# Graph attention on one core: the order of TensorE's transposes, and of the last graph's work, is changed

## The chip, the core and the metric

The kernel runs on one core of a Trainium2 chip. The metric is the time on the device in microseconds (us), lower is better. A core has TensorE (PE in the rows, its weight loads PEld), VectorE (DVE), ScalarE (ACT), GpSimd (POOL) and SyncE (SP, which here only issues DMAs), each with its own queue of instructions, worked through in order. Semaphores order the engines among each other.

## The reference

For each of 32 graphs of 256 nodes with 256 features and 8 heads of 32, all in float32:

```python
q, k, v = (proj(Wq, bq), proj(Wk, bk), proj(Wv, bv))
scores = jnp.einsum('bhqd,bhkd->bhqk', q, k) * SCALE
mask = (adj_matrix + bond_matrix)[:, None, :, :]      # both are adj: 2 * adj
attn = jax.nn.softmax(scores * mask, axis=-1)
ctx = jnp.einsum('bhqk,bhkd->bhqd', attn, v)
y = jnp.einsum('bse,fe->bsf', ctx, Wo) + bo           # ctx with heads side by side
x = _layernorm(x + y, axis=-1)
```

## The kernel before

The work is a software pipeline over the 32 graphs. Each engine has a function `step(g)`, called for g = 0 to 31, and a tail that is written out by hand behind it. In step g TensorE makes the scores of graph g, while the sums over the values belong to graph g − 2 and the output projection to graph g − 3.

A graph's eight heads are two groups of four; group n is 2g or 2g + 1. For a group:

- TensorE makes the scores (`rows`, L265: 16 matmuls of 32 rows each, four heads side by side in the array) into four PSUM banks `row_bank`.
- VectorE multiplies them by the mask, writes `probs` and the row maxima `top` (`reduce_rows`, L524). GpSimd negates the maxima (`lower_tops`, L934), and ScalarE takes the exponential with them as bias, and sums the rows (`exp`, L729).
- The sums over the values need the probabilities turned. Three heads of a group are turned in 32 by 32 blocks on VectorE (`box`, L537) and carried across partitions by four DMAs from SyncE (`carry_boxes`, L209) into `carried`. The fourth head, "the head" in this text, is turned on TensorE (`turn_probs`, L282: four transposes into `turn_bank`) and moved to `turned_probs` by ScalarE (`move_turned`, L737).
- `weigh_v` (L405: 32 matmuls of 32 columns each) sums over the values into `ctx_bank`. It waits for the boxes of both groups and for both moved heads.

The sums of the exponentials become shares: VectorE takes the reciprocal (`divide`, L545), GpSimd spreads them over 512 columns (`spread_shares`, L870, into `wide`), TensorE turns them (`turn_shares`, L367, four transposes, also into `turn_bank`), and ScalarE copies them to `inverse` (`copy_inverse`, L743). VectorE multiplies sums and shares (`scale_context`, L552), GpSimd cuts the product into a high and a low part (`cut_context`, L878 and L880), and TensorE projects it (`project_out`, L422, 12 matmuls) into `out_bank`. VectorE adds the residual (`add_residual`, L558; GpSimd has added the bias to it, `add_bias`, L887), takes the statistics (L566, L572), and GpSimd normalises (`make_scale`, L894 to L903, `normalise`, L910). ScalarE issues the store (`store`, L788) and the loads of masks and residuals (`load_masks`, `load_x`).

Beside that TensorE projects two graphs ahead: per step two of the four projections for k and q of a pair (`project_kq`, L334, 6 matmuls, into `proj_bank`, read by ScalarE in `read_kq`, L757), and v of the next graph (`project_v`, L352). There are 16 pairs, so that steps 30 and 31 have no `project_kq`.

`turn_bank` has four users in a row: the second-group head of graph g − 1 and the first-group head of graph g, each followed by ScalarE's move, and the shares, followed by ScalarE's copy. `turn_probs` and `turn_shares` wait for the move or the copy before them (L278, L279, L364). So TensorE's order in a step is scores, projection, output projection, shares, sums, head, scores, projection, v, head.

For the last graph nothing is carried. All its eight heads are turned on TensorE (`turn_last`, L287), moved by ScalarE or VectorE (`move_last`), summed half by half, scaled, cut, projected and normalised in halves (`scale_last`, `high_last`, `low_last`, `project_last`, `add_last`, `normalise_last`). Both engines' copies are counted by `last_moved_act` and `last_moved_dve`, for which `weigh_v(LAST)` waits.

Of the kernel before, what the change touches and what calls it, by code (L numbers as in the profile page):

```python
# [35 lines left out]
LAST = B - 1  # L36
# [4 lines left out]
def build(nc, x, x_t, adj, adj_t, wq, wk, wv, wo, bq, bk, bv, bo, out):  # L41
    ctx = ExitStack()
    with ctx:
# [206 lines left out]
        def _(pe):  # L250
# [121 lines left out]
            def weigh_v(g):  # L372
# [6 lines left out]
                if g == LAST:  # L379

                    pe.wait_ge(last_moved_act, 3)
                    pe.wait_ge(last_moved_dve, 5)
                else:

                    wait(pe, ctx_ready, g)
                    pe.wait_ge(moved, 2 * g + 2)
                    for n in range(T * g, T * g + T):
                        pe.wait_ge(carried_in[n % 4], 64 * (n // 4 + 1))
# [79 lines left out]
            def step(g):  # L468
# [7 lines left out]
                if g == 1:  # L476
                    make_bias()
                if is_graph(g - 3):
                    project_out(g - 3)
                if is_graph(g - 2):  # L480
                    turn_shares(g - 2)
                    weigh_v(g - 2)
                turn_probs(2 * g - 1)
# [25 lines left out]
        def _(dve):  # L509
# [172 lines left out]
            for g in range(B):  # L682
                step(g)
            aggregate(LAST - 3)
            for j in (2, 3):
                move_last(0, j)
# [3 lines left out]
            move_last(1, 2)  # L690
            add_residual(LAST - 2)
# [20 lines left out]
        def _(act):  # L712
# [96 lines left out]
            def step(g):  # L809
                ahead = g // 2 + 1  # L810
                for s in range(H):
                    n, j = 2 * g + s // J, s % J
                    if s == 0 and is_graph(g - 2):
                        copy_inverse(g - 2)
# [14 lines left out]
                    if s == (6 if g < LAST else 1) and is_graph(g):  # L829
                        load_x(g)  # L830
                    if s == (3 if g > 0 else 4) and is_pair(ahead):
                        read_kq(ahead, 2 * (g % 2) + 1)
# [4 lines left out]
                    if s in (3, 4) and g == LAST:  # L837
                        move_last(0, s - 3)
                    if s == 7 and is_pair((g + 1) // 2 + 1):
                        read_kq((g + 1) // 2 + 1, 2 * ((g + 1) % 2))  # L840
# [3 lines left out]
            move_last(1, 3)  # L844
            store(LAST - 4)
            copy_inverse(LAST)
# [8 lines left out]
        def _(pool):  # L855
# [81 lines left out]
            def step(g):  # L937
# [3 lines left out]
                if is_graph(g - 1):  # L941
                    spread_shares(g - 1)
                    if g % 2 == 0:
                        add_bias((g - 1) // 2, 1)
                if is_graph(g - 2):
                    cut_context(g - 2)
                lower_tops(2 * g + 1)
                if g % 2 == 1:
# [9 lines left out]
            add_bias(LAST // 2, LAST % 2)  # L958
            make_scale(LAST - 3)
            normalise(LAST - 3)  # L960
            spread_shares(LAST)
            cut_context(LAST - 1)
            make_scale(LAST - 2)
# [48 lines left out]
```

## Time and profile before

| | |
|---|---|
| time before, median of 3 runs | 404.72 us |
| lowest and highest | 403.47 and 408.22 us |
| the profiled execution, its own time | 409.81 us |
| its span, first to last instruction | 408.0 us |
| mean granted TensorE clock | 0.988 |
| busy: PE, PEld, DVE, ACT, POOL | 94%, 72%, 89%, 89%, 67% |
| mean DMA rate | 226 GB/s |

The profiled execution is longer than the median of the three. Its rows have times in microseconds from the span's start. A timeline row has the start, the length from the first start to the last end of what it merges, engine, source line, operation, tile written and tiles read, the shape and the count; in brackets the idle time of the engine before it and what ended it. TensorE's matmuls are pipelined, so that the blocks overlap by some 0.1 to 0.2 us and their starts tell more than their ends.

### The profile page before, as it was taken

To read this page: it belongs to the slowest core of one execution; us is meant where nothing else is said; L and a number is where in the kernel's file an instruction comes from. 1 tells how busy PE (TensorE), PEld (TensorE's weight loads), DVE (VectorE), ACT (ScalarE), POOL (GpSimd) and SP (SyncE) were. 2 spreads that over 40 slices of the span, in tenths; PEclk is the share of its full clock that TensorE was granted. 3 is DMA by queue.
4 is the path that set the end of the run, shared out by engine and by line. 5 is a ranking of instruction groups with operands and counts; after the bars stand their busy time and mean duration, and the time that the engine had idled before them with its cause. 6 is when DMAs were issued, how large, how long until landed. Compare 5 with 4: busy or idle time off the path is not lost.

```text
span 408.0 us, 12272 instructions
## 1 busy us (share of the span) xinstructions
PE 382.6 (94%) x3628; PEld 293.5 (72%) x3628; DVE 364.4 (89%) x1336; ACT 362.4 (89%) x1223; POOL 272.8 (67%) x507
## 2 busy tenths in 40 slices
PE   8999999999999999999999999899999899996872
PEld 7766777877777777777777776677777677775632
DVE  4998899999899999899999988899999899999655
ACT  4699999999899999999999998899999899998810
POOL 3245647777586777768777775768777587475583
PEclk9999999999999999999999999999999999999968
DMA  8478888888999998889899889998988888887603
GB/s 271 135 199 246 223 236 241 247 216 224 270 269 241 255 258 233 254 228 272 241 259 243 225 204 247 261 250 250 261 240 217 220 246 225 224 223 193 174 26 104
DMA packets 65428, 92.30 MB, mean 226 GB/s; under 512 B 8529, under 2 KB 48722, under 8 KB 65362
## 3 DMA queue, kind: packets, MB, share of 16 engines
q1 hardware_dynamic: 47426, 66.35, 62.3%
q10 hardware_dynamic: 17936, 25.17, 19.5%
q8 instruction: 29, 0.48, 0.4%
q14 instruction: 37, 0.30, 0.2%
HBM read 26.22 MB, written 8.39 MB: 85 GB/s over the span
## 4 chain that ended last, share of the span: by engine, by line
PE 48%; SPq 22%; DVE 8%; DMA 8%; ACT 5%; issue 5%; POOL 2%; DVEq 0%; POOLq 0%
SPq L209 13%; PE proj_bank L334 11%; PE ctx_bank L405 9%; SPq L218 9%; PE row_bank L265 9%; DMA carried<-boxes 8%; PE out_bank L422 5%; PE out_bank L352 5%; PE turn_bank L282 5%; ACT probs L729 4%; DVE probs L524 4%; DVE boxes L537 2%; PE turn_bank L367 2%; PE turn_bank L454 1%; ACT kq L757 1%
## 5 line engine op out<-in xcount | busy, mean ns | idle before, releaser
L729 ACT ACTIVATE probs<-probs,low_top 128x256 f32<-128x256 f32 x512 | 254.6, 506 | 4.3 <-POOL low_top L934 4.3
L524 DVE CUSTOM_DVE_ANT_0 probs<-row_bank,adj_rows 128x256 f32<-128x256 f32 x512 | 181.1, 420 | 22.0 <-issue 12.6
L537 DVE STREAM_TRANSPOSE boxes<-probs 128x1536 f32<-128x1536 f32 x62 | 108.9, 1757 | 0.0
L729 ACT ACTIVATION_READ_ACCUMULATOR probs<-probs,low_top 128x1 f32 x512 | 100.5, 196 | 0.0
L334 PE MATMUL proj_bank<-xt_parts,w_parts 128*128 128x512 f32 x360 | 99.7, 412 | 0.0
L334 PEld LDWEIGHTS proj_bank<-xt_parts,w_parts 128*128 128x128 f32 x360 | 62.9, 188 | 30.8 <-issue 19.6
L934 POOL TENSOR_SCALAR low_top<-top 128x4 f32<-128x4 f32 x128 | 25.3, 198 | 79.3 <-issue 36.0
L265 PE MATMUL row_bank<-kq 32*128 32x256 f32 x1024 | 73.3, 400 | 1.5 <-DVE top L524 1.5
L405 PE MATMUL ctx_bank<-carried,v_boxed 128*32 128x256 f32 x744 | 59.6, 383 | 8.3 <-DMA carried<-boxes 8.1
L265 PEld LDWEIGHTS row_bank<-kq 32*128 32x128 f32 x1024 | 46.4, 184 | 13.7 <-issue 11.8
L422 PEld LDWEIGHTS out_bank<-w_parts,ctx_parts 128*128 128x128 f32 x372 | 48.8, 191 | 5.1 <-issue 2.7
L352 PEld LDWEIGHTS out_bank<-w_parts,xt_parts 128*128 128x128 f32 x384 | 50.3, 190 | 2.9 <-issue 0.3
L352 PE MATMUL out_bank<-w_parts,xt_parts 128*128 128x256 f32 x384 | 51.3, 283 | 0.0
L422 PE MATMUL out_bank<-w_parts,ctx_parts 128*128 128x256 f32 x372 | 50.3, 285 | 1.1 <-issue 1.1
L405 PEld LDWEIGHTS ctx_bank<-carried,v_boxed 128*32 128x32 f32 x744 | 29.6, 109 | 28.1 <-issue 14.0
L737 ACT COPY turned_probs<-turn_bank 128x512 f32<-128x512 f32 x62 | 36.2, 585 | 7.6 <-PE turn_bank L282 7.4
L524 DVE DVE_READ_ACCUMULATOR2_ANT top<- 128x1 f32 x512 | 42.8, 84 | 0.0
L880 POOL TENSOR_TENSOR ctx_parts<-context,ctx_parts 128x512 fp32r<-128x512 f32 x31 | 40.2, 1298 | 2.5
L887 POOL TENSOR_TENSOR xr<-xr,bias 128x512 f32<-128x512 f32 x32 | 41.0, 1281 | 0.0
L864 POOL TENSOR_TENSOR xt_parts<-xt,xt_parts 128x512 fp32r<-128x512 f32 x30 | 38.9, 1297 | 2.6
L282 PE MATMUL turn_bank<-ident,probs 128*128 128x128 f32 x248 | 39.1, 280 | 1.2 <-ACT probs L729 0.7
L282 PEld LDWEIGHTS turn_bank<-ident,probs 128*128 128x128 f32 x248 | 27.3, 141 | 14.5 <-ACT probs L729 10.9
(85 smaller groups left out, 436.9 us busy)
## 6 DMA issues: line engine op xcount, KB each, us to landing
carried<-boxes SPq DMA_DIRECT2D x248, 192.0 KB, 3.9
xt<-in_x_t SPq DMA_DIRECT2D x32, 256.0 KB, 4.7
adj_rows<-in_adj ACTq DMA_DIRECT2D x32, 256.0 KB, 3.5
xr<-in_x ACTq DMA_DIRECT2D x32, 256.0 KB, 4.4
v_boxed<-v SPq DMA_DIRECT2D x124, 64.0 KB, 3.4
out<-result ACTq DMA_DIRECT2D x31, 256.0 KB, 4.5
w_whole<-in_wk ACTq DMA_DIRECT2D x2, 128.0 KB, 3.5
w_whole<-in_wq SPq DMA_DIRECT2D x1, 256.0 KB, 4.2
```

Source lines behind the costliest of these rows:

```text
L209: sp.dma_start(carried[:, g % 2, c, i].rearrange("p h f -> p (h f)"), boxes[D * i:D * (i + 1), n % BOXES].rearrange("p j h f -> p j (h f)" ...
L265: last = nc.tensor.matmul(row_bank[j][:, t * S:(t + 1) * S], kq[own, pair % 2, 2 * c + 1, b * S + t * P:b * S + (t + 1) * P], kq[own, pair ...
L282: last = nc.tensor.transpose(turn_bank[:, c * S + t * P:c * S + (t + 1) * P], probs[:, (J * n + J - 1) % RING, t * S + c * P:t * S + (c + ...
L334: last = nc.tensor.matmul(proj_bank[:], w_parts[:, a, which, t, c * P:(c + 1) * P], xt_parts[:, pair % 2, b, t, :], start=(half_ == 0 and ...
L352: last = nc.tensor.matmul(out_bank[:, tile * E:(tile + 1) * E], xt_parts[:, (n // 2) % 2, a, t, nodes], w_parts[:, c, 2, t, :], start=(til ...
L405: last = nc.tensor.matmul(place.rearrange("p (u i q) -> p u i q", u=T, i=J), values[:, (g // 2) % 2, g % 2, t, o * D:(o + 1) * D], tile, s ...
L422: last = nc.tensor.matmul(out_bank[:, n * E:(n + 1) * E], ctx_parts[:, g % 2, a, f, nodes], w_parts[:, b, 3, f, :], start=(n == 0 and i == 0),
L524: last = nc.vector.tensor_tensor_reduce(probs[:, h % RING, t * S:(t + 1) * S], row_bank[j][:, t * S:(t + 1) * S], adj_rows[:, (g // 2) % 2 ...
L537: nc.vector.transpose(boxes[:, n % BOXES].rearrange("p a h (f q) -> p (h f) a q", q=D), probs[:, first:first + BOXED, :].rearrange("p h (f ...
L729: last = nc.scalar.activation(tile, tile, ACT.Exp, bias=low_top[:, g % 2, J * c + j, t:t + 1], accum_out=sums[:, g % 2, t, j * T + c:j * T ...
L880: nc.gpsimd.tensor_tensor(low, context[:], high.bitcast(F32), ALU.subtract).then_inc(ctx_low, 1)
L887: nc.gpsimd.tensor_tensor(tile, tile, bias[:].unsqueeze(1).to_broadcast([P, T, E]), ALU.add).then_inc(x_ready, 1)
```

## The change

Three things change, and nothing of what is computed.

TensorE's step: `turn_shares(g - 2)` moves ahead of `project_out(g - 3)`, and `turn_probs(2 * g - 1)` ahead of `weigh_v(g - 2)`. The order is then scores, projection, shares, output projection, head, sums, scores. ScalarE follows: `copy_inverse` is issued at the end of the step before, behind the last exponentials and ahead of `read_kq`, where it was behind `read_kq`.

The loads and biases of the last residuals: `load_x(LAST)` is issued in step 30, and both `add_bias` of the last pair come in step 31 ahead of `cut_context(g - 2)` and the second tops.

The tail: VectorE turns to `move_last(0, 2)` and the residual of graph 29 earlier, and `move_last(1, 2)` goes from VectorE to ScalarE, so TensorE waits for four copies of each. GpSimd spreads the last shares and cuts the context of graph 30 ahead of `normalise(LAST - 3)`.

```diff
@@ tensor: weigh_v
-                    pe.wait_ge(last_moved_act, 3)
-                    pe.wait_ge(last_moved_dve, 5)
+                    pe.wait_ge(last_moved_act, 4)
+                    pe.wait_ge(last_moved_dve, 4)
@@ tensor: step
+                if is_graph(g - 2):
+                    turn_shares(g - 2)
                 if is_graph(g - 3):
                     project_out(g - 3)
+                turn_probs(2 * g - 1)
                 if is_graph(g - 2):
-                    turn_shares(g - 2)
                     weigh_v(g - 2)
-                turn_probs(2 * g - 1)
                 rows(2 * g + 1)
@@ vector: tail
+            move_last(0, 2)
             aggregate(LAST - 3)
-            for j in (2, 3):
-                move_last(0, j)
+            add_residual(LAST - 2)
+            move_last(0, 3)
             for j in (0, 1):
                 move_last(1, j)
             divide(LAST)
-            move_last(1, 2)
-            add_residual(LAST - 2)
             scale_context(LAST - 1)
@@ scalar: step
-                    if s == 0 and is_graph(g - 2):
-                        copy_inverse(g - 2)
...
-                    if s == (6 if g < LAST else 1) and is_graph(g):
+                    if s == 6 and g < LAST:
                         load_x(g)
+                    if s == 7 and g == LAST - 1:
+                        load_x(LAST)
...
+                    if s == 7 and is_graph(g - 1) and g < LAST:
+                        copy_inverse(g - 1)
                     if s == 7 and is_pair((g + 1) // 2 + 1):
                         read_kq((g + 1) // 2 + 1, 2 * ((g + 1) % 2))
@@ scalar: tail
-            move_last(1, 3)
+            for j in (2, 3):
+                move_last(1, j)
+            copy_inverse(LAST)
             store(LAST - 4)
-            copy_inverse(LAST)
@@ gpsimd: step
+                if g == LAST:
+                    for b in range(2):
+                        add_bias(LAST // 2, b)
                 if is_graph(g - 2):
                     cut_context(g - 2)
                 lower_tops(2 * g + 1)
-                if g % 2 == 1:
+                if g % 2 == 1 and g < LAST:
                     add_bias((g - 1) // 2, 0)
@@ gpsimd: tail
-            add_bias(LAST // 2, LAST % 2)
             make_scale(LAST - 3)
-            normalise(LAST - 3)
             spread_shares(LAST)
             cut_context(LAST - 1)
+            normalise(LAST - 3)
             make_scale(LAST - 2)
```

## Rows read from the trace of the kernel before

**Rows 1.** The waits from 50 to 350 us: engine and line, total, times, longest.

```profile
PE ctx_bank L405 <- DMA carried<-boxes: 6.6, 8, 1.4
```

**Rows 2.** The waits of SyncE's DMA queue in the same stretch.

```profile
SPq L209 <- DVE boxes L537: 16.8, 19, 1.9
```

**Rows 3.** The timeline of TensorE in step 29, from first scores to the next step's.

```profile
348.83 1.15 PE L265 MATMUL row_bank<-kq 32*128 32x256 f32 x16
349.90 1.68 PE L334 MATMUL proj_bank<-xt_parts,w_parts 128*128 128x512 f32 x6
351.42 1.58 PE L422 MATMUL out_bank<-w_parts,ctx_parts 128*128 128x256 f32 x12
352.84 0.60 PE L367 MATMUL turn_bank<-ident,wide 128*128 128x128 f32 x4
353.37 1.27 PE L405 MATMUL ctx_bank<-carried,v_boxed 128*32 128x256 f32 x18
...
354.92 0.39 PE L405 MATMUL ctx_bank<-turned_probs,v 128*32 128x256 f32 x2
355.24 0.66 PE L282 MATMUL turn_bank<-ident,probs 128*128 128x128 f32 x4
355.82 1.15 PE L265 MATMUL row_bank<-kq 32*128 32x256 f32 x16
356.90 1.65 PE L334 MATMUL proj_bank<-xt_parts,w_parts 128*128 128x512 f32 x6
...
360.36 1.15 PE L265 MATMUL row_bank<-kq 32*128 32x256 f32 x16
```

**Rows 4.** The timeline of ScalarE in the same stretch, without the exponentials.

```profile
350.08 0.58 ACT L737 COPY turned_probs<-turn_bank 128x512 f32<-128x512 f32 x1
...
352.54 0.68 ACT L757 ACTIVATE kq<-proj_bank,b_k 128x512 f32<-128x512 f32 x1
353.48 0.59 ACT L743 COPY inverse<-turn_bank 128x512 f32<-128x512 f32 x1 [0.26 <-PE turn_bank L367]
...
358.59 0.69 ACT L757 ACTIVATE kq<-proj_bank,b_q 128x512 f32<-128x512 f32 x1
```

**Rows 5.** The timeline of GpSimd in the tail.

```profile
386.34 1.11 POOL L910 TENSOR_SCALAR result<-y,scale 128x256 f32<-128x256 f32 x2
387.41 1.28 POOL L887 TENSOR_TENSOR xr<-xr,bias 128x512 f32<-128x512 f32 x1
...
391.46 0.61 POOL L870 COPY wide<-shares 128x512 f32<-128x512 f32 x1
```

**Rows 6.** The timeline of TensorE in step 31 and the tail.

```profile
376.42 1.27 PE L405 MATMUL ctx_bank<-carried,v_boxed 128*32 128x256 f32 x18 [1.30 <-DMA carried<-boxes]
...
384.71 0.60 PE L304 MATMUL turn_bank<-ident,probs 128*128 128x128 f32 x4
385.15 1.69 PE L304 MATMUL row_bank<-ident,probs 128*128 128x128 f32 x12
...
388.63 0.66 PE L304 MATMUL row_bank<-ident,probs 128*128 128x128 f32 x4
392.12 1.11 PE L367 MATMUL turn_bank<-ident,wide 128*128 128x128 f32 x4 [2.83 <-POOL wide L870]
```

**Rows 7.** Windows: stretch, its length, busy of the five engines, PEclk, DMA share, GB/s.

```profile
392.00:398.00 6.00, 5.88 (x42) 3.36 (x43) 1.41 (x4) 1.40 (x3) 4.28 (x9) 0.50 0.00 0
```

**Rows 8.** The timeline of TensorE in step 2: the head.

```profile
36.68 0.63 PE L282 MATMUL turn_bank<-ident,probs 128*128 128x128 f32 x4 [0.52 <-ACT inverse L743]
```

**Rows 9.** The timeline of ScalarE in step 2: the copy of the shares.

```profile
35.94 0.60 ACT L743 COPY inverse<-turn_bank 128x512 f32<-128x512 f32 x1
```

**Rows 10.** The timeline of VectorE in the tail.

```profile
387.68 1.28 DVE L580 COPY carried<-row_bank 128x512 f32<-128x512 f32 x2
388.87 0.24 DVE L545 RECIPROCAL shares<-sums 128x16 f32<-128x16 f32 x1
...
399.17 0.69 DVE L558 TENSOR_TENSOR y<-out_bank,xr 128x512 f32<-128x512 f32 x1 [0.97 <-PE out_bank L422]
```

## What the change does to the time: the prediction

> **What bounds the kernel now.** I read the page first, for the engines' shares, then the waits of the middle 300 us, then the timeline of one undisturbed step, engine by engine, then the timeline of the end. TensorE, VectorE and ScalarE are all nearly full by the page, so what counts is which of them the others wait for. In the middle TensorE itself waits for one thing that the profile names, the boxes carried by DMA: 6.6 us in 8 waits between 50 and 350 us [rows 1]. SyncE's queue in its turn waited for the boxes 19 times in that stretch, 16.8 us in all [rows 2], so in most of the 25 steps it caught up with its work. It is close to full, and a late box is a queue's lateness, which comes and goes.
>
> [rows 3] is one whole step (`g` = 29) without such a wait. The starts of TensorE's blocks: first scores 348.83, projection 349.90, output projection 351.42, turned shares 352.84, sums 353.37, turned head 355.24, second scores 355.82, and the next step at 360.36. A step is 11.53 us, and no gap stands in it that another engine made: TensorE sets the pace. ScalarE runs just behind [rows 4]: it is through with the head's exponentials at 352.54, reads a projection, stands 0.26 us until the turned shares are there, and copies them from 353.48 to 354.07. It meets TensorE again at 358.59, when the second projection has ended (355.82 + 1.08 + 1.65 = 358.55). So from the second scores to the copy of the shares it keeps a fixed distance to TensorE.
>
> The end is another regime. The last graph's shares are spread on GpSimd at 391.46, after two residual biases and two normalisations [rows 5]; TensorE stands for 2.83 us and goes on at 392.12 [rows 6] at half the clock, 0.50 from 392 to 398 us [rows 7], which is 1.2 GHz.
>
> **Part 1: the order on TensorE in a step.** Nothing is computed more or less; blocks change places. What changes is the switch between matmuls on the whole array and those on a quarter of it (scores 32*128, sums 128*32). Four transposes cost 0.53 us ahead of the sums (353.37 − 352.84) and 0.58 between sums and scores (355.82 − 355.24) [rows 3], but 0.44 when a whole-array block follows (385.15 − 384.71) [rows 6]. Before, from the projection to the second scores: 1.52 + 1.42 + 0.53 + 1.87 + 0.58 = 5.92. After, with shares, output projection, head, sums: 1.52 + 0.44 + 1.42 + 0.53 + 1.87 = 5.78. That is 0.14 us less a step. Its weak term is the last, sums straight into scores, which the trace does not have. The sums go in 8 rounds of four, (354.92 − 353.37) / 7 = 0.22 apart, and the head comes 0.32 after the last round's start. If the scores follow at the sums' own pitch, the 1.87 is 1.77 and the gain 0.24. I take 1.87: the scores' weights need all 128 columns, which the last sums still use.
>
> The Trainium skill, "TensorEngine Tiling (Array Packing)", section Tiling Modes, says that a change of tiling mode, not merely of tile, drains TensorE. By it sums into scores is still a change of mode: 1.87 stands, and the step has one such change less; without the rule it would be 1.77.
>
> **Part 2: who must now be in time.** The turned head goes into the bank that the shares were in, so it waits for ScalarE's copy of them. Before, the sums (1.87 us) lay between and hid this; now the output projection does, 1.42 us. In the old step's times TensorE is ready for the head at 349.90 + 1.52 + 0.44 + 1.42 = 353.28. ScalarE has the copy right behind the exponentials now, ahead of the projection's read: 352.54 + 0.59 = 353.13 [rows 4], and TensorE starts 0.14 after such a copy has ended (35.94 + 0.60 to 36.68) [rows 8, 9]: 353.27. That is a tie, and as ScalarE's distance to the second scores is fixed, it is one in every step. A weight load that has to wait is not drawn ahead either, 0.05 us (0.58 against 0.53). Bounds: 0 and 0.15 us a step in 27 steps; I take 0.5 us in all, near the lower end. A gain is excluded, since it is a wait.
>
> The shares, 1.42 us earlier, need the move of the head before: 350.08 + 0.58 = 350.66, against 351.42 [rows 3, 4]: 0.76 us to spare, nothing. ScalarE's projection read comes behind the copy, but the 0.26 of standing goes, and the exponentials queued behind both start earlier than now. VectorE's product of sums and shares gets its sums 0.4 us later; it is behind a transpose then, and ahead of the mask of the second scores, which needs scores that end later still. GpSimd's cut and SyncE's queue get no new wait in front of them.
>
> **Part 3: the carried boxes.** The sums start 0.44 us later behind the projection than now, and the step is 0.14 shorter. Boxes are pinned to the second scores of two steps before, so the allowance grows by 0.30 us. Eight waits at 0.30 are 2.4 us, ten over the run 3.0; nothing if SyncE's queue, which has 0.14 us less a step to catch up, gives it back. I take 1.2.
>
> **Part 4: the start.** In step 2 ScalarE is still a microsecond behind and there is no output projection. TensorE does the sums first, then the head waits for the copy until 36.68 [rows 8, 9]. After, the copy is ahead of the projection's read, some 0.57 earlier, head at 36.11, then 0.53 + 1.87 until the scores: 38.51, against 36.68 + 0.58 = 37.26. It is 1.25 later, of which step 3 gives back some, since ScalarE has then caught up. Cost 1.1 (bounds 0 and 1.3).
>
> **Part 5: the end.** Steps 30 and 31 have no projection, so the shares wait for the move and the head for the copy, in the open; against that the sums of step 31, which stand 1.30 us for boxes now [rows 6], come late enough not to. I put the last scores 0.5 earlier than now. On GpSimd both residual biases (1.28 us each) lie ahead of the last tops; the load that the second needs is issued a step earlier, so it is there. The normalisation of graph 27 ends at 386.34 + 1.11 = 387.45 now [rows 5], and at 387.45 − 1.28 − 0.5 = 385.65 after. VectorE's residual (0.69) waits for it, then come three copies (1.28 for two) and the reciprocal (0.24) [rows 10]: 385.65 + 0.6 + 1.9 + 0.2 = 388.35 at the most, 388.1 with the overlaps of the pipeline. The normalisation of graph 28 no longer stands ahead of the spread: + 0.1 + 0.61 = 388.8. TensorE's last head ends at 388.63 + 0.66 − 0.2 = 389.1 [rows 6]. So the shares turn at 389.1 instead of 392.12: 3.0 us. TensorE then never stands for 2.8 us, so the granted clock should stay at 2.4 GHz. ScalarE copies the last head (0.58 and 0.14) until 389.8, sums 1.87, output projection 1.42 and 0.3 until VectorE takes it: 393.4, against 399.17 now [rows 10]. From the shares to that residual it was 7.05 us and is 4.3: 2.75 more. Behind it all is as now. Together 5.75 us; 3.0 if the clock falls all the same.
>
> **Sum.** 1.1 − 27 × 0.14 (3.8) − 1.2 + 0.5 − 5.75 = −9.15 us against the profiled execution's span of 408.0: 398.9. That execution took 409.8 us by its own time, 5 us over the median of 404.72. I put the difference to waits for boxes, so the median has fewer of them to save: 0.5 instead of 1.2. 404.72 − 8.45 = 396.3, rounded to 396.5.
>
> **Rivals.** (a) *ScalarE's copy is late.* For it the tie above; against it that TensorE itself fixes the copy's place. At 0.15 us a step the steps gain nothing: 3.5 more, 400.0. Chance 0.13. (b) *The DMA side keeps the pace.* Each step carries the same bytes. SyncE's idle time is 16.8 us in 25 steps [rows 2], 0.67 a step, of which 0.14 is taken; so it has room. If it gives back all that the steps save, the end is left and half of the start: 404.7 − 5.75 + 0.5 = 399.5. Chance 0.1. (c) *The clock falls in the tail anyway:* 396.5 + 2.75 = 399.3. Chance 0.1. (d) *Sums flow into scores:* 27 × 0.10 less, 393.8. Chance 0.08. (e) *Slower: the head's wait for the copy grows.* If shares and copy come later than the rows say, every step pays on TensorE with all engines behind it. 8.45 / 27 = 0.31 us a step cancels the gain; 0.46 makes it 1% slower, 408.8. For it: VectorE and ScalarE have under 0.5 us a step to absorb anything. Against it: 0.31 is twice my upper bound. Chance 0.04. The forecast has 0.55.
>
> **How the numbers follow.** Under 1% a measurement of this kernel can't tell from no change. The predicted time is the forecast's; the range reaches below (d), and over (a), (b) and (c): 393.2 to 401.2. Faster by over 1% is below 400.7: the forecast, (c), (d), most of (a) and (b), 0.84. Slower by over 1% has 0.04, within 1% the remaining 0.12.
>
> **What would show it.** In an undisturbed step: a period of 11.39 instead of 11.53; the head right behind the output projection; no idle time ahead of the copy of the shares; sums to scores 1.87 (or 1.77). Fewer than 8 waits for boxes in the same stretch. A wait of TensorE for `inverse` in each step shows (a) or (e). In the tail: shares turned 3 us sooner, seen from the start of step 30, and a granted clock of 1.00 to the last matmul. I would be wrong above all by block lengths that no row has, and by VectorE's chain from the normalisation to the reciprocal.

## The result: slower, by 2.6%

| | before | after |
|---|---|---|
| median of 4 runs each, us | 406.26 | 417.5 |
| lowest to highest, us | 403.47 to 408.22 | 412.85 to 418.01 |
| profiled execution, time / span, us | 409.81 / 408.0 | 417.26 / 415.5 |

The ratio after to before is 1.0256, with a 95% interval of 1.0154 to 1.0359, so it is slower beyond the noise. Medians here and below take all runs of a kernel, while ratios leave out runs over 1.5% above the fastest of their kernel, so the two can differ by over 1%. The forecast was 396.5 us.

The page of after shows the change of regime at once. First line: span. Then the engines' busy time and the chain that ended last, share by engine:

```profile
span 415.5 us, 12272 instructions
PE 378.0 (91%) x3628; PEld 293.3 (71%) x3628; DVE 365.8 (88%) x1335; ACT 360.2 (87%) x1224; POOL 272.9 (66%) x507
...
SPq 55%; PE 21%; issue 5%; DMA 5%; ACT 5%; DVE 4%; POOL 3%; DVEq 0%; POOLq 0%
```

SyncE's DMA queue now holds 55% of that chain, where it held 22% before and TensorE 48%. The waits from 50 to 350 us (engine and line, total, times, longest):

```profile
ACT kq L757 <- PE proj_bank L334: 27.4, 24, 3.9
...
PE ctx_bank L405 <- DMA carried<-boxes: 18.1, 17, 2.0
```

and those of SyncE's queue in the same stretch:

```profile
SPq L209 <- DVE boxes L538: 2.4, 4, 1.2
```

TensorE waits for carried boxes 17 times and 18.1 us instead of 8 times and 6.6 [rows 1]. SyncE waited for the boxes 19 times, 16.8 us, before [rows 2]; now 4 times, 2.4 us. So it hardly ever catches up: what it is late with goes on into the next step.

Yet a step without such a wait is the one that was forecast. TensorE in step 29 (start, length, engine, line, operation, output and inputs, shape, count), the counterpart of [rows 3]:

```profile
360.93 1.15 PE L265 MATMUL row_bank<-kq 32*128 32x256 f32 x16
362.01 1.66 PE L334 MATMUL proj_bank<-xt_parts,w_parts 128*128 128x512 f32 x6
363.50 0.60 PE L367 MATMUL turn_bank<-ident,wide 128*128 128x128 f32 x4
363.86 1.67 PE L422 MATMUL out_bank<-w_parts,ctx_parts 128*128 128x256 f32 x12
365.36 0.62 PE L282 MATMUL turn_bank<-ident,probs 128*128 128x128 f32 x4
365.92 1.27 PE L405 MATMUL ctx_bank<-carried,v_boxed 128*32 128x256 f32 x18
...
367.78 1.15 PE L265 MATMUL row_bank<-kq 32*128 32x256 f32 x16
...
372.32 0.93 PE L265 MATMUL row_bank<-kq 32*128 32x256 f32 x12
```

Its period is 372.32 − 360.93 = 11.39 us, and sums to scores take 367.78 − 365.92 = 1.86. But over steps 6 to 28 the period is 12.31 us in the mean, from 11.38 to 15.07; it was 11.85 before. Step 30 starts at 372.32 instead of 360.36: 12.0 us lost. From there to the end it takes 43.2 us instead of 47.6: 4.5 won back. That is the +7.5 of the spans; by the medians it is 11.2, since before's profiled execution was longer than its median by 3.5.

**What moved that the forecast had not followed.** ScalarE in the same step, its DMA issues among its work (ACTq), the counterpart of [rows 4]:

```profile
364.64 0.57 ACT L743 COPY inverse<-turn_bank 128x512 f32<-128x512 f32 x1
364.75 0.41 ACTq L788 DMA_DIRECT2D out<-result  x1
365.11 0.69 ACT L757 ACTIVATE kq<-proj_bank,b_k 128x512 f32<-128x512 f32 x1
366.22 0.33 ACTq L716 DMA_DIRECT2D adj_rows<-in_adj  x1
367.65 0.58 ACT L737 COPY turned_probs<-turn_bank 128x512 f32<-128x512 f32 x1
```

The issue of the masks' load (256 KB) stands in ScalarE's queue behind `move_turned(2 * g - 1)`, so it goes out once TensorE has turned that head. Before, the rows of step 29 were

```profile
353.49 0.40 ACTq L788 DMA_DIRECT2D out<-result  x1
...
355.94 0.34 ACTq L716 DMA_DIRECT2D adj_rows<-in_adj  x1
```

with first scores at 348.83 [rows 3]: store at 4.66 us in the step, load at 7.11. After, with first scores at 360.93: 3.82 and 5.29. Over steps 6 to 28 the medians are 4.66 and 7.11 before, 4.24 and 5.30 after. The load comes 1.8 us earlier, right behind the store of 256 KB. From issue to landing (minimum, median, maximum, between 50 and 350 us) the load took 3.1, 3.5, 4.0 us before and the store 3.8, 4.6, 5.3. After, first the load, then the store:

```profile
DMA to landing us min/median/max: 4.6/6.0/7.2
```

```profile
DMA to landing us min/median/max: 4.7/5.9/7.1
```

What SyncE does meanwhile depends on how late it is. Where it is on time it issues the values (`v_boxed`, L218) in this stretch: over steps 6 to 28 they begin at 5.0 us of a step before and 4.8 in e10 below (medians), and are through at 8.7 and 7.6. In after they begin at 7.2 and end at 11.2, because the queue is late with the boxes ahead of them. The store's and the load's transfers, issued at 4.24 and 5.30 and 6 us long, reach from the boxes' issues into the values'. SyncE in step 15 of after, whose first scores are at 187.45:

```profile
186.48 3.06 SPq L209 DMA_DIRECT2D carried<-boxes  x4
189.58 1.12 SPq L200 DMA_DIRECT2D xt<-in_x_t  x1
190.80 3.13 SPq L209 DMA_DIRECT2D carried<-boxes  x4
194.03 4.13 SPq L218 DMA_DIRECT2D v_boxed<-v  x4
198.25 3.09 SPq L209 DMA_DIRECT2D carried<-boxes  x4
201.39 0.68 SPq L200 DMA_DIRECT2D xt<-in_x_t  x1
```

and ScalarE's issues in the same step:

```profile
192.39 0.44 ACTq L788 DMA_DIRECT2D out<-result  x1
...
193.19 0.69 ACTq L716 DMA_DIRECT2D adj_rows<-in_adj  x1
```

Store and load are issued among the boxes, right ahead of the values' issues, which take 4.13 us for four, and SyncE goes from one group to the next without a pause. Over steps 6 to 28 issuing the values took 3.54 us a step before and 3.87 after, the boxes 6.28 and 6.94: a microsecond more a step in a queue that had 0.67 us to spare by [rows 2]. With the load of `xt` it is 10.44 us a step before and 11.47 after, which is more than after's undisturbed step of 11.39: such a queue cannot keep up. The Trainium skill, "DMA: Bandwidth & Descriptors", section Issuing engines are not separate DMA queues, says that transfers of all issuing engines run on the same DMA engines and interleave. The trace agrees as to the landing times; that also the issue on another queue gets longer is what the trace adds.

### The profile page after: what moved, and what is told of

The parts are those of the page before. It is cut to its first block, busy times and chain, and to the rows that moved or that the text cites. A ratio compares the mean times of both kernels' runs of the same rounds, so it can differ in the third digit from the quotient of the medians.

```text
span 415.5 us, 12272 instructions
## 1 busy us (share of the span) xinstructions
PE 378.0 (91%) x3628; PEld 293.3 (71%) x3628; DVE 365.8 (88%) x1335; ACT 360.2 (87%) x1224; POOL 272.9 (66%) x507
## 4 chain that ended last, share of the span: by engine, by line
SPq 55%; PE 21%; issue 5%; DMA 5%; ACT 5%; DVE 4%; POOL 3%; DVEq 0%; POOLq 0%
SPq L209 33%; SPq L218 19%; PE ctx_bank L405 5%; PE proj_bank L334 5%; PE row_bank L265 4%; ACT probs L729 4%; DMA carried<-boxes 4%; SPq L200 3%; PE out_bank L352 2%; PE out_bank L422 2%; DVE probs L525 2%; PE turn_bank L282 1%; DVE boxes L538 1%; DMA xt<-in_x_t 1%; POOL result L913 1%
## 5 line engine op out<-in xcount | busy, mean ns | idle before, releaser
L525 DVE CUSTOM_DVE_ANT_0 probs<-row_bank,adj_rows 128x256 f32<-128x256 f32 x512 | 181.1, 419 | 15.6 <-PE row_bank L265 11.9
L405 PE MATMUL ctx_bank<-carried,v_boxed 128*32 128x256 f32 x744 | 61.1, 389 | 18.8 <-DMA carried<-boxes 18.7
L937 POOL TENSOR_SCALAR low_top<-top 128x4 f32<-128x4 f32 x128 | 25.3, 197 | 73.1 <-issue 47.7
L405 PEld LDWEIGHTS ctx_bank<-carried,v_boxed 128*32 128x32 f32 x744 | 31.8, 110 | 38.1 <-issue 25.6
L422 PE MATMUL out_bank<-w_parts,ctx_parts 128*128 128x256 f32 x372 | 51.6, 288 | 0.0
L422 PEld LDWEIGHTS out_bank<-w_parts,ctx_parts 128*128 128x128 f32 x372 | 46.0, 189 | 0.4 <-issue 0.4
L757 ACT ACTIVATE kq<-proj_bank,b_q 128x512 f32<-128x512 f32 x30 | 20.6, 688 | 28.5 <-PE proj_bank L334 28.5
L881 POOL CAST ctx_parts<-context 128x512 fp32r<-128x512 f32 x31 | 19.0, 613 | 38.5 <-DVE context L553 38.4
L282 PE MATMUL turn_bank<-ident,probs 128*128 128x128 f32 x248 | 38.1, 276 | 3.4 <-ACT inverse L743 2.6
```

The costliest lines, as they stand in the source:

```text
L282: last = nc.tensor.transpose(turn_bank[:, c * S + t * P:c * S + (t + 1) * P], probs[:, (J * n + J - 1) % RING, t * S + c * P:t * S + (c + ...
L405: last = nc.tensor.matmul(place.rearrange("p (u i q) -> p u i q", u=T, i=J), values[:, (g // 2) % 2, g % 2, t, o * D:(o + 1) * D], tile, s ...
L422: last = nc.tensor.matmul(out_bank[:, n * E:(n + 1) * E], ctx_parts[:, g % 2, a, f, nodes], w_parts[:, b, 3, f, :], start=(n == 0 and i == 0),
L525: last = nc.vector.tensor_tensor_reduce(probs[:, h % RING, t * S:(t + 1) * S], row_bank[j][:, t * S:(t + 1) * S], adj_rows[:, (g // 2) % 2 ...
```

## The experiments

Ratios are to the kernel before in the same sitting, whose medians lay between 403.9 and 406.0 us; intervals are 95%. The sittings were on three chips, and before's own median moves by 2 us between them; so do not read a difference of 2 us between kernels of different sittings. "Moment" is the median time of an issue from its step's first scores; "waits" are TensorE's waits for carried boxes from 50 to 350 us.

### Which part costs

**e3: the end alone**, in the old order of the step.

```diff
@@ vector, scalar, gpsimd: tails; load_x(LAST), add_bias
+  as in the change
@@ tensor: step; scalar: copy_inverse in step
   as before
```

> The kernel before with the change's edits from step 30 on alone: load of the last residual, biases, order of the tail on VectorE, ScalarE and GpSimd. The steps' order on TensorE and ScalarE is that of before. By the two traces the stretch from step 30 to the end is 4.5 us shorter in the changed kernel (43.2 against 47.6): 400 to 402 us. If the tail's gain hangs on the order of the steps, 404 to 406.

Measured: 402.3 us, ratio 0.9922 (0.9875 to 0.997); waits 5.3 us in 6. The new end is worth 3 to 4 us by the times. By the traces it is more: from step 30's start to the end e3 takes 42.0 us, before 47.6; 1.30 of the 5.7 are a wait for boxes in before's step 31 [rows 6].

**e4: the step's order alone**, with the old end.

```diff
@@ tensor: step; scalar: copy_inverse in step
+  as in the change
@@ all tails, load_x, add_bias
   as before
```

> The change's order of a step alone (shares ahead of the output projection, head ahead of the sums, copy of the shares ahead of the projection's read), the tail as before. Both theories: the whole loss is here, 416 to 422 us, more than the changed kernel's own 417.5 less 4.5 for its tail and with some 15 us more than before by step 30.

Measured: 421.75 us, ratio 1.0403 (1.0332 to 1.0475); waits 15.6 us in 11. The loss is in the order of the step, and it is larger than what the new end returns.

**e8: only the shares first**; the head is turned behind the sums again.

```diff
@@ tensor: step
-                turn_probs(2 * g - 1)
                 if is_graph(g - 2):
                     weigh_v(g - 2)
+                turn_probs(2 * g - 1)
```

> The changed kernel with the head turned behind the sums again; the shares stay ahead of the output projection, and ScalarE's copy of them ahead of the projection's read. The turned head comes at about 7 us again, and with it the load of the masks, since ScalarE's queue waits for the head ahead of it. The step is about 11.5 us. Theory A: 400 to 404 us. Theory B, since the step is as long as before: also 400 to 404 us. If the loss comes from the shares' and the copy's place, 412 us or more.

Measured: 403.96 us (median of 10) beside 405.31 before, ratio 1.0068 (1.0013 to 1.0123); the ratio stands on the other side of 1 than the medians, so "about the same" is all that can be said. Waits 3.2 us in 5, masks at 7.11, store at 4.24, shortest period 11.50. The half of the change that moves the head is the half that costs, and with it goes the masks' moment.

**e7: is it that the step is short?** After, with two more transposes in each step, so that SyncE has more time a step and not less.

```diff
@@ tensor: turn_probs, behind the waits
+                if n % 2 == 0 and n > 0:
+                    for c in range(T):
+                        nc.tensor.transpose(turn_bank[:, c * S:c * S + P],
+                            probs[:, (J * n + J - 1) % RING, c * P:(c + 1) * P], ident[:])
```

> The changed kernel with two more transposes on TensorE in each step (they repeat two of the first head's, so the result is the same): a step without waits is 11.6 us instead of 11.39, longer than before's 11.53. Masks and store go out as in the changed kernel. Theory A: nothing is gained, 416 to 420 us. Theory B: SyncE's queue can catch up again, waits for boxes fall to those of before, 402 to 408 us.

Measured: 420.18 us, ratio 1.0416 (1.0306 to 1.0525). An undisturbed step is 11.57 to 11.60 us, longer than before's 11.51, and the waits are still 10.9 us in 11, with store and load at 4.02 and 5.10. The short step by itself is not the cause.

### The moment of the masks' load

**e1: the load one place later** in ScalarE's queue.

```diff
@@ scalar: step
-                    if s == 2 and is_graph(g + 2):
-                        load_masks(g + 2)
+                    if s == 3 and is_graph(g + 2):
+                        load_masks(g + 2)
```

> The changed kernel with one edit: ScalarE issues the load of the masks behind the fourth exponential of a step instead of behind the third. In the changed kernel that load went out 5.3 us after a step's first scores, 1.06 us behind the store; before it was 7.11 us and 2.45 us. Theory A (the load of the masks has moved onto the store, and the two together hold up SyncE's queue): issue at 6.3 to 6.8 us, landing of masks and stores back under 5 us, SyncE's issues of boxes back towards 6.3 us a step, and a time of 397 to 403 us. Theory B (the shorter step leaves SyncE's queue no time to catch up, whatever ScalarE loads): no change, 412 to 418 us.

Measured: 413.35 us, ratio 1.0203 (1.0152 to 1.0254); moment 6.28, waits 11.3 us in 10. Load and store landed after 4.5 and 4.9 us (medians), as theory A had it, and yet the time lies in theory B's range and 10 us over theory A's. The load went only half of the way to 7.1. This run could not decide between the two; e7 and e5 do.

**e5: the load back at its old moment.** ScalarE's queue waits for the sums before it issues it.

```diff
@@ scalar: step
                     if s == 2 and is_graph(g + 2):
+                        if is_graph(g - 2):
+                            act.wait_ge(ctx_made, g - 1)
                         load_masks(g + 2)
```

> The changed kernel, with ScalarE waiting for the sums of the step before it issues the load of the masks. It then goes out about 7.0 us after a step's first scores, as in the kernel before, and later when TensorE waits for boxes, also as before. Theory A (the moment of that load and its distance from the store do the harm; at 6.28 us a third of the loss was gone): waits for boxes near those of before, 398 to 404 us. Theory B (the step of 11.39 us is too short for SyncE's queue): still 410 to 414 us.

Measured: 405.03 us (median of 10), ratio 0.9999 (0.9949 to 1.0048); moment 6.99; waits 6.2 us in 8, SyncE's own 13.3 us in 19. TensorE's order is that of after, and the loss against before is gone; e6, which turned out to be the same kernel in effect, measured 407.85 (ratio 1.0125). At 405 to 408 instead of 417.5 this shows that the loss hangs on when the load goes out. The range of theory A, 398 to 404, was still too low.

**e2: the early load in the old order.**

```diff
@@ scalar: step
-                    if s == 2 and is_graph(g + 2):
+                    if s == 1 and is_graph(g + 2):
                         load_masks(g + 2)
```

> The kernel before with one edit: the load of the masks stands ahead of the move of the turned head, so that it doesn't wait for the head any more. Order of TensorE, tail and all else as before. Theory A: the load goes out about 1 us behind the store as in the changed kernel, masks and stores take 5.5 to 6 us to land, more and longer waits for boxes, 411 to 420 us. Theory B: TensorE's step is as long as before, so 403 to 408 us, as before.

Measured: of ten runs four took 403.1 to 405.3 us and six 411.5 to 420.8; the median is 411.61. The ratio, 0.9977 (0.9926 to 1.0027), goes by the four, and by it the early load costs the old order nothing, where theory A had 411 to 420. Why the six are longer is not shown; before's runs beside them lie between 402.0 and 411.1. In the trace, of a run of 411.53 us, the moment is 5.26 with the store at 4.66, landing takes 5.6 us (median), and the waits are 7.5 us in 11, hardly more than before's 6.6 in 8. So this run does not support the cause. It limits it: that a load at 5.3 near a store costs 12 us is shown in the new order alone, and what of the new order it needs (the store at 4.24 instead of 4.66, or the order itself) is open.

**e9: the load after the values**, at 8 us.

```diff
@@ scalar: step
-                    if s == 2 and is_graph(g + 2):
-                        load_masks(g + 2)
...
+                    if s == 3 and is_graph(g + 2):
+                        act.wait_ge(rows_made, 2 * g + 2)
+                        load_masks(g + 2)
```

> The changed kernel, with the load of the masks issued behind the fourth exponential and only when the second scores are made, about 8.1 us after a step's first scores and 3.9 us behind the store: three transfers of ScalarE's nearly even over the step. If more distance from the store helps further, 399 to 403 us; if what the gate at 7.0 us gave (405.0) was all there is, 403 to 407; if the load must also keep clear of the boxes that SyncE issues from about 8 us on, 408 or more.

Measured: 407.84 us (median of 10), ratio 1.0045 (0.9988 to 1.0102); moment 8.07, waits 5.3 us in 9. A load at 8 us does not do better than one at 6.99 in e5. With the store left at 4.2 some waits stay.

**e11: the same in the old order**, with the new end.

```diff
@@ scalar: step (over e3)
-                    if s == 2 and is_graph(g + 2):
-                        load_masks(g + 2)
...
+                    if s == 3 and is_graph(g + 2):
+                        act.wait_ge(rows_made, 2 * g + 2)
+                        load_masks(g + 2)
```

> The order of a step as before, the tail of the change, and the masks' load issued at about 8.1 us as in the first kernel of this set (3.4 us behind the store at 4.66). Against the tail alone (402.3 us, masks at 7.1 us): 399 to 402 if spacing helps, 402 to 404 if 2.45 us behind the store were enough already.

Measured: 405.28 us (median of 10), ratio 1.002 (0.9972 to 1.0068), against 0.9922 for e3, and over both ranges expected. In the trace, which is of the longest of the ten runs (411.1 us), the load fell at 8.52, the waits are 9.6 us in 15, and the mean period was 12.0. Later is not better for the load in this order either.

### The store

**e6: the store one place later** (over e5).

```diff
@@ scalar: step
-                    if s == 0 and is_graph(g - 5):
+                    if s == 1 and is_graph(g - 5):
                         store(g - 5)
```

> As the run with the gated masks, and the store is issued one head later too (about 5.2 us after the first scores, where the changed kernel has 4.24 and the kernel before 4.66). Theory A in its wider form (each of ScalarE's transfers has to meet few boxes): within 2 us of the gated masks, either way; if the store's 0.4 us is what is left of the loss, 4 us or more faster than it. Theory B: 410 to 414 us.

Measured: 407.85 us, ratio 1.0125 (1.0019 to 1.0231). The store still went out at 4.25, so the edit did not move it: one exponential more ahead of it does not hold the queue. It decides nothing about the store. What it gives is a second measurement of e5's kernel, 3 us over the first, with waits of 9.0 us in 12.

**e10: the store away from the values**, the load left where the change put it.

```diff
@@ scalar: step
-                    if s == 0 and is_graph(g - 5):
-                        store(g - 5)
+                    if s == 3 and is_graph(g - 5):
+                        act.wait_ge(rows_made, 2 * g + 2)
+                        store(g - 5)
```

> The changed kernel, with the masks' load left where the change put it (5.3 us) and the store moved away instead: issued behind the fourth exponential when the second scores are made, about 8.1 us, 2.8 us behind the masks. If the harm is that store and masks stand together, 402 to 407 us. If it is the masks' load at 5.3 us in itself, against SyncE's values and boxes, 414 to 419 us.

Measured: 395.9 us (395.43 to 398.46), ratio 0.9769 (0.9715 to 0.9822). This beats both kernels, and lies under both ranges expected. The chain that ended last, by engine:

```profile
PE 84%; ACT 8%; POOL 3%; issue 2%; DVE 1%; DMA 1%; DVEq 0%; POOLq 0%; ACTq 0%
```

TensorE has no wait for carried boxes left between 50 and 350 us, and SyncE's queue has 26 of its own:

```profile
SPq L209 <- DVE boxes L538: 23.3, 26, 2.0
```

Step 16 (first scores 191.78), ScalarE's issues and then SyncE's:

```profile
197.07 0.33 ACTq L716 DMA_DIRECT2D adj_rows<-in_adj  x1
199.84 0.40 ACTq L788 DMA_DIRECT2D out<-result  x1
```

```profile
193.23 3.22 SPq L209 DMA_DIRECT2D carried<-boxes  x4
196.54 2.58 SPq L218 DMA_DIRECT2D v_boxed<-v  x4
```

The load still goes out among the values, at 5.29 us, but alone; the store follows at 8.06, when they are through. Four values take 2.58 us here, not 4.13; over steps 6 to 28 the values take 2.76 us a step and the boxes 6.64, with `xt` 9.90 in all. Every step from 6 to 28 takes 11.38 to 11.41 us.

**e14: both late and near each other**, load at 6.99 and store at 8.06, in the new order.

```diff
@@ scalar: step (over e10)
                     if s == 2 and is_graph(g + 2):
+                        if is_graph(g - 2):
+                            act.wait_ge(ctx_made, g - 1)
                         load_masks(g + 2)
```

> The changed kernel with the masks' load at 7.0 us (behind the sums) and the store at 8.1 us (behind the second scores), 1.07 us apart as in the changed kernel, but 3 us later in the step. If nearness harms wherever it is, 410 us or more; if it is the store at 4.2 us among SyncE's values, 395 to 399 us.

Measured: 399.08 us, ratio 0.9897 (0.9856 to 0.9939), waits 1.0 us in 3. The two are 1.07 us apart, as in after (1.06), and hardly a wait is left. Of the 3.2 us over e10 about 1.6 are half clock behind a stand in step 2 (last section), which e10's trace does not have. So it is not their nearness by itself that costs, but where in SyncE's round they lie.

**e12: the old order, new end, store at 8.19**, load at its old 7.10; and **e13: the same with the load at 4.68**, the old order's counterpart of e10.

```diff
@@ scalar: step (e12, over e3)
-                    if s == 0 and is_graph(g - 5):
-                        store(g - 5)
...
+                    if s == 3 and is_graph(g - 5):
+                        act.wait_ge(rows_made, 2 * g + 2)
+                        store(g - 5)
@@ scalar: step (e13, over e12)
-                    if s == 2 and is_graph(g + 2):
+                    if s == 1 and is_graph(g + 2):
                         load_masks(g + 2)
```

> The order of a step as before, the change's tail, and the store issued when the second scores are made (8.1 us); the masks' load stays at 7.1 us, so that the two are 1 us apart. If nearness is what harms, 408 us or more; if the store's moment at 4.7 us harms, waits for boxes go and the time is 397 to 400 us.

> As the kernel before this in the set, with the masks' load at 5.3 us too: ScalarE's transfers at the moments of the kernel that took 395.9 us, with the step's order of before and the change's tail. Without waits for boxes step 30 starts at 360.4 - 7.6 = 352.8 us, against 351.4 in that kernel: 397 to 398.5 us, so that the order of the step is worth 1 to 2.5 us. If the new order is what takes the waits away, 402 or more.

Measured: e12 400.6 us (median of 10), ratio 0.9906 (0.9871 to 0.9941), waits 0.9 us in 3. e13 398.65 us, ratio 0.9898 (0.9851 to 0.9944), waits 1.4 us in 3, shortest period 11.51. The late store takes the waits away in the old order too, but what that gains in time against e3 (ratio 0.9922) is not clear of the noise. And e13 beside e10 gives what TensorE's new order is worth when the queue isn't in the way: 2.75 us by the medians, some 5 by the ratios, which come from two sittings, and 3.2 us by the start of step 30 (354.55 against 351.37), of which 1.4 are e13's waits.

Time is the median of all runs, ratio that to before in the same sitting.

| kernel | order | load | store | waits, us | time, us | ratio |
|---|---|---|---|---|---|---|
| before | old | 7.11 | 4.66 | 6.6 | 406.26 | 1 |
| e2 | old | 5.26 | 4.66 | 7.5 | 411.61 | 0.9977 |
| e3 | old, new end | as before | as before | 5.3 | 402.3 | 0.9922 |
| e11 | old, new end | 8.52 | 4.66 | 9.6 | 405.28 | 1.002 |
| after | new | 5.30 | 4.24 | 18.1 | 417.5 | 1.0256 |
| e8 | new, old head | 7.11 | 4.24 | 3.2 | 403.96 | 1.0068 |
| e1 | new | 6.28 | as after | 11.3 | 413.35 | 1.0203 |
| e5 | new | 6.99 | 4.24 | 6.2 | 405.03 | 0.9999 |
| e9 | new | 8.07 | 4.25 | 5.3 | 407.84 | 1.0045 |
| e14 | new | 6.99 | 8.06 | 1.0 | 399.08 | 0.9897 |
| e10 | new | 5.30 | 8.07 | 0 | 395.9 | 0.9769 |
| e12 | old, new end | 7.10 | 8.19 | 0.9 | 400.6 | 0.9906 |
| e13 | old, new end | 4.68 | 8.20 | 1.4 | 398.65 | 0.9898 |

## Why the prediction was wrong

**The step that failed** is the last sentence of part 2: "GpSimd's cut and SyncE's queue get no new wait in front of them." It is true of semaphores. But I had listed what is queued behind ScalarE's copy, which the change moves, and not what is queued behind its move of the turned head, whose moment moves with the head. An issue of 256 KB stands there. Before, the head was turned at 355.24, 6.4 us into the step [rows 3]; after, at 365.36, 4.4 us in. The load follows it, 7.11 to 5.30, and its transfer lies beside SyncE's issues together with the store's. What the runs showed in place of "no new wait" is a queue whose issues took 1 us a step longer, and 18.1 us of waits for boxes instead of 6.6. The trace of before could have told: the issue's moment was there to be read, and that it follows the head is in the code.

**Rival (b) had the right place and the wrong mechanism.** It said that the DMA side keeps the pace, and counted bytes a step and SyncE's idle time, with the lengths of SyncE's issues taken as fixed. The bytes did not change, so on its terms the queue could do no more than give back the steps' gain. What changed was how long SyncE's own issues take when others' transfers lie beside them: 1 us a step more, against 0.67 of slack. Rival (e), the only slower one, put the loss at the head's wait for the copy; that wait is 1.8 us, once, at the start, none between 50 and 350, and 0.8 behind. With 0.04 for slower the text had no room for what happened.

**Part 1 was right.** Undisturbed period 11.38 to 11.41 (11.39 forecast), sums to scores 1.86 (1.87). With it rival (d), sums that flow into the scores at 1.77, falls. Those 27 × 0.14 us are in the kernel; they show in e10, whose steps all take this long.

**Part 2's tie held exactly.** The copy of the shares ends at 364.64 + 0.57 = 365.21, and the head starts at 365.36, 0.15 behind it and right behind the output projection; no idle time ahead of the copy. It costs nothing that can be seen, where I had 0.5. Rival (a) falls.

**Part 3 had the wrong sign.** Forecast: waits for boxes shrink by 1.2 us (0.5 for the median). Measured: idle time ahead of the sums from 8.3 to 18.8 us over the run. The allowance of 0.30 us follows from the blocks' starts; the boxes came later by more.

**Part 4.** The second scores of step 2 came 1.29 us later than before, seen from its first scores (7.86 us against 6.57); the forecast was 1.25, of which step 3 was to give some back. It didn't: step 3 begins 1.68 us later than before, 0.41 of which was there in step 1. So about 1.3, not 1.1. And that is the cheap case: the stand of TensorE for the copy in step 2, 1.82 us long, was followed by half clock in six of the nine traces that have it (e1, e4, e6, e7, e9, e14), and then step 2 takes 14.0 us instead of 12.4. The forecast had no such term.

**Part 5, the end,** came out nearly as worked out, seen from the start of step 30 at 372.32:

```profile
385.51 0.63 PE L367 MATMUL turn_bank<-ident,wide 128*128 128x128 f32 x4 [0.89 <-ACT turned_probs L737]
...
389.24 1.27 PE L405 MATMUL ctx_bank<-carried,v_boxed 128*32 128x256 f32 x18 [0.65 <-DMA carried<-boxes]
...
391.10 1.15 PE L265 MATMUL row_bank<-kq 32*128 32x256 f32 x16
...
400.87 0.66 PE L304 MATMUL row_bank<-ident,probs 128*128 128x128 f32 x4
401.92 0.66 PE L367 MATMUL turn_bank<-ident,wide 128*128 128x128 f32 x4 [0.40 <-POOL wide L873]
402.51 1.07 PE L405 MATMUL proj_bank<-carried,v 128*32 128x256 f32 x16
...
404.37 1.68 PE L422 MATMUL out_bank<-w_parts,ctx_parts 128*128 128x256 f32 x12
```

TensorE stands 0.40 us for the spread, not 2.83 [rows 6]. The shares turn 29.6 us after step 30's start; it was 392.12 − 360.36 = 31.76, and 3 us less was forecast: 28.75. The missing 0.85 is there already when GpSimd ends the normalisation of graph 27, as its rows and VectorE's show:

```profile
397.31 1.11 POOL L913 TENSOR_SCALAR result<-y,scale 128x256 f32<-128x256 f32 x2
...
401.26 0.61 POOL L873 COPY wide<-shares 128x512 f32<-128x512 f32 x1 [1.16 <-DVE shares L546]
```

```profile
398.55 0.69 DVE L559 TENSOR_TENSOR y<-out_bank,xr 128x512 f32<-128x512 f32 x1 [0.99 <-POOL result L913]
...
400.95 0.24 DVE L546 RECIPROCAL shares<-sums 128x16 f32<-128x16 f32 x1
```

The normalisation ends at 398.42, 26.1 us after step 30's start, where 385.65 − 360.36 = 25.3 was forecast. GpSimd does wait 1.16 us for the reciprocal, but VectorE's chain to it, which I had named as what could be wrong, takes 2.8 us from there, about the 2.5 to 2.7 worked out. Late is what comes ahead of it. "I put the last scores 0.5 earlier" failed: they begin 18.8 us after step 30's start (391.10), and 18.5 before (378.87 − 360.36), since the sums of step 31 still stood 0.65 us for boxes. Where the boxes are in time, as in e10, the last scores begin at 18.1 and the end takes 42.2 us.

The clock held, as forecast; the window that answers to [rows 7] (stretch, length, busy of five engines, granted clock, DMA share, GB/s):

```profile
404.00:410.00 6.00, 3.47 (x34) 2.90 (x24) 4.60 (x15) 0.81 (x2) 4.89 (x12) 1.00 0.31 106
```

Rival (c) falls. Together 4.5 us of 5.75 in the trace of after, 5.4 in e10's and 5.7 in e3's; by the times e3 has 3.7 (medians) or 3.2 (ratio).

**The sum, with the cause removed.** e10 is the change without its collision: 395.9 us, where 396.5 was forecast. That is partly luck. Against before in its own sitting e10 wins 9.1 us. The order of the step brought 2.75 us by the medians (e13 to e10; forecast, with 0.5 for the boxes, 3.8 − 0.5 + 0.5 − 1.1 = 2.7), though other readings of the same pair go up to 5, and the end 3 to 4. What is left is e10's late store, which also takes away the waits that before had of its own (e3 to e13: waits 5.3 to 1.4), and of which the forecast knew nothing; its size in time is not clear of the noise.

**Where after's 20.9 us against e10 lie.** Step 30 starts at 372.3 in after and at 351.4 in e10. Of the 20.9, 18.1 are idle time for boxes ahead of the sums, and about 1.5 are one spell of half clock (below). That leaves 1.3 us, so nothing else of size is hidden in the steps.

**What stays open.** Shown is, for the new order: with the load at 5.3 the store's moment decides (after, e10); with the store at 4.2 the load's moment decides (after, e1, e5); at 4.2 and 5.3 together they cost most. In the old order the early load alone cost nothing by the ratio (e2), and the reason for the difference is open. Not shown is why the store at 4.2 keeps some waits alive with the load at 7 or 8 (e5, e9), while the load at 5.3 with the store at 8 keeps none (e10). No run has the store or the load with nothing else beside it. That the DMA engines push back on SyncE's issues is read from the issues' lengths, and is argued, not isolated: moving SyncE's values instead was not tried.

## What to carry to other kernels

When a block is moved on one engine, list every instruction that its consumer's queue holds behind the consuming one, DMA issues first, and write down the new moment of each. In a kernel whose DMA engines are busy most of the time (0.89 of each 100 us from 50 to 350 before, 0.86 to 0.88 after, 0.90 to 0.92 in e10) moments count, not only bytes: these and the issue counts stayed the same while one transfer of 256 KB came 1.8 us earlier, near another, and SyncE's issues took 1 us more a step. And a queue with 0.67 us of slack in 11.5 is a bound in waiting: before an order is judged on such a kernel, add up the queue's issues of a step and compare the sum with the new step (here 11.47 against 11.39), and try the moments of the loads and stores beside it.

## What the runs showed of the hardware

**The length of a DMA issue went with when other queues' transfers ran.** A value's issue on SyncE took 0.60 us in the median before, 0.70 after, and 0.60 in e10, with up to 2.3 us before, 2.6 in after and 1.6 in e10 (line L218, 50 to 350 us; minimum, median, maximum in ns; first after, then e10):

```profile
L218 SPq DMA_DIRECT2D v_boxed<-v x97: 547/695/2585, 50.0 to 346.5; - x97
```

```profile
L218 SPq DMA_DIRECT2D v_boxed<-v x105: 507/597/1621, 49.7 to 347.2; - x105
```

The bytes are the same in both, and the kernels differ only in the store's moment; that SyncE's own issues then fall elsewhere too is not separated. The mean rate went from 226 GB/s before to 222 after and 235 in e10: in after the DMA engines moved less per second than in e10, while SyncE's queue was late.

**A stand of 2 us was sometimes followed by half clock.** In step 9 of after TensorE stood 1.98 us for boxes and then ran the sums at the lower level (0.57 over 120 to 124 us, that is mostly 1.2 GHz):

```profile
120.35 2.18 PE L405 MATMUL ctx_bank<-carried,v_boxed 128*32 128x256 f32 x18 [1.98 <-DMA carried<-boxes]
...
123.77 1.22 PE L265 MATMUL row_bank<-kq 32*128 32x256 f32 x16
```

```profile
118.00:120.00 2.00, 0.37 (x4) 0.13 (x2) 2.00 (x5) 1.96 (x8) 1.84 (x5) 1.00 0.84 225
120.00:124.00 4.00, 3.65 (x36) 2.04 (x40) 0.62 (x2) 2.74 (x11) 0.91 (x2) 0.57 1.00 265
```

The sums took 3.4 us instead of 1.86. Here a wait of 1.98 us cost another 1.5. The other sixteen waits of after between 50 and 350 us, none longer than 2.0, show no such spell. Other runs go both ways: e4's waits for boxes of 2.44 and 4.17 us and e7's of 2.06, 2.18 and 2.31 had a stretch at 0.5 that began within 1 us of their end, e1's of 2.73 and e2's of 2.13 had none. The 1.82 us in step 2 of the new order had half clock behind them in six of nine traces. Such a spell costs about 1.6 us by step 2 (14.0 against 12.4), and it can lie in one kernel's trace and not in another's that is compared with it.
